# The stack's fills issued piece by piece in the attention stages of a two-layer model kernel

## What is computed

```python
x = L0_attn_x                                   # 16 x 256 x 128
xn = _layernorm(x)
s = _L0_attn_ref(xn, ...)                       # causal, 16 heads, the difference of two softmaxes, head norm
g = _silu(_L0_ffn_ref(xn, ...))                 # 8 experts, top 2, with a capacity
x = x + s * g
xn = _layernorm(x)
s = _L1_attn_ref(xn, ...)                       # 16 heads, a window of 128, with biases
g = _silu(_L1_ffn_ref(xn, ...))                 # 8 experts, top 2
x = x + s * g
```

## Time and profile before

| what | us |
|---|---|
| time, three executions | 1351.52, 1352.54, 1356.94 |
| median | 1352.54 |
| span of the profiled execution, first to last instruction | 1353.5 |
| attention of layer 0, from its first instruction | about 231 to 790 |
| attention of layer 1 | about 979 to 1353 |

### The profile page before, as it was taken

One profiled execution on the slowest core, in us unless ns is written; L12 is line 12 of the kernel. 1 busy time (PEld: TensorE's weight loads), 2 busy tenths in 40 slices (PEclk: granted clock), 3 DMA queues, 4 the chain that ended last, 5 costly groups with the idle time before them and its releaser, 6 DMA issues. The chain is left out here.

```text
span 1353.5 us, 38128 instructions
## 1 busy us (share of the span) xinstructions
PE 1071.2 (79%) x12376; PEld 808.5 (60%) x12376; DVE 809.8 (60%) x1668; ACT 799.8 (59%) x1892; POOL 615.5 (45%) x918
## 2 busy tenths in 40 slices
PE   4359998588999798899987344999857888978885
PEld 3349998355565455556554244999824655655553
DVE  4676664568777577777751357666436664755641
ACT  4845555057777677777776342655514665656663
POOL 6256553023455456555665416655303242444443
PEclk9999999579999899999998555999958898989997
DMA  6402222322332222232200340222212122222210
GB/s 181 113 24 69 70 69 47 93 56 58 85 77 58 58 57 65 67 85 68 57 20 9 94 109 16 71 69 68 55 47 63 44 64 66 55 62 64 52 48 20
DMA packets 144615, 86.43 MB, mean 64 GB/s; under 512 B 16547, under 2 KB 138037, under 8 KB 144469
## 3 DMA queue, kind: packets, MB, share of 16 engines
q1 hardware_dynamic: 135828, 66.72, 18.9%
q0 software_dynamic: 8640, 17.71, 5.6%
HBM read 30.06 MB, written 15.60 MB: 34 GB/s over the span
## 5 line engine op out<-in xcount | busy, mean ns | idle before, releaser
L1424 DVE TENSOR_REDUCE at_maxima<-ps 128x2 f32<-128x512 f32 (+1 forms) x576 | 371.7, 683 | 226.3 <-PE ps L1117 223.9
L1313 ACT ACTIVATE at_probs<-ps 128x512 f32<-128x512 f32 x576 | 320.8, 598 | 108.8 <-PE ps L1117 104.2
L1116 PE MATMUL ps<-tables 64*128 64x256 bf16 (+1 forms) x2304 | 229.6, 260 | 128.9 <-DMA stack<-at_pieces 62.3
L1117 PE MATMUL ps<-stack 62*128 62x256 bf16 (+3 forms) x3072 | 265.6, 255 | 2.4 <-issue 2.4
L717 ACT ACTIVATE ex_hid<-ps,ex_w 128x128 f32<-128x128 f32 x568 | 162.0, 368 | 120.3 <-PE ps L690 111.2
L1116 PEld LDWEIGHTS ps<-tables 64*128 64x128 bf16 x2304 | 91.7, 96 | 229.7 <-issue 193.9
L646 POOL DMA_INDIRECT ex_rows<-xn_rows,ex_ids_now x142 | 143.7, 1012 | 110.4 <-PE ps L681 68.7
L1117 PEld LDWEIGHTS ps<-stack 62*128 62x128 bf16 (+1 forms) x3072 | 167.1, 99 | 13.7 <-issue 2.6
L750 DVE COPY ex_w<-weights 128x1156 f32 x142 | 109.3, 769 | 103.8 <-issue 102.8
L1005 POOL DMA_INDIRECT at_chosen_y<-list_out,at_slot x128 | 130.1, 1017 | 55.3 <-issue 29.0
L690 PE MATMUL ps<-ex_rowsT,ex_w 128*128 128x128 f32 x1136 | 154.8, 281 | 0.0
(11 more groups left out here) (188 smaller groups left out, 1504.2 us busy)
## 6 DMA issues: line engine op xcount, KB each, us to landing
stack<-at_pieces SPq DMA_DIRECT2D x192, 128.0 KB, 2.7
stack<-at_pieces SPq DMA_DIRECT2D x192, 64.0 KB
list_out<-ex_result SPq DMA_DIRECT2D x142, 64.0 KB, 1.5
weights<-in_L_w SPq DMA_DIRECT2D x4, 1024.0 KB, 5.6
weights<-in_L_w SPq DMA_DIRECT2D x16, 256.0 KB, 6.6
xn_rows<-xn SPq DMA_DIRECT2D x8, 512.0 KB, 3.3
ex_rows<-xn_rows,ex_ids_now POOLq DMA_INDIRECT x142, 2.6
x<-in_L_attn_x SPq DMA_DIRECT2D x4, 512.0 KB, 6.1
```

The costliest lines, as they stand in the source:

```text
L1116: return nc.tensor.matmul(fine(bank, j), R.eye[tile, j, :], mask[tile], start=(j == 0), stop=True, skip_group_check=(j > 0))
L1117: return nc.tensor.matmul(bank[:, j - 2, :], left(j - 2)[tile], right(j - 2)[tile], start=False, stop=True, skip_group_check=True)
L1313: nc.scalar.activation(probs[:, (n // 3) % 2, n % 3, i * 512:(i + 1) * 512], t_bank[i], ACT.Exp, scale=SCALE).then_inc(t_free, 1)
L1424: nc.vector.tensor_reduce(by_half[:, h0:h0 + heads, a], s_bank[i].rearrange("p (m k) -> p m k", k=P * (late + 1)), AX.X, ALU.max).then_inc ...
```

## The change

SyncE no longer issues the twelve DMAs of a fill together behind the third piece. `fill_stack` becomes `fill_pieces`, called three times a step. Piece 0's six DMAs wait for ScalarE's copy of the second projection (`g_free`), and for all DMAs of earlier fills (`stacked`). Piece 1's four wait for VectorE's second split operation (`split_chain`), piece 2's two for the third (`pieces_ready`). In layer 1 piece 0 stands ahead of the shift in SyncE's order, in layer 0 behind it; in layer 1 the store comes between pieces 1 and 2. The other engines' programs stay as they are.

```diff
-            def fill_stack(b, r):
+            def fill_pieces(step, b, r, piece):
 
                 pieces = pieces_of[r % 2]
-                lone_wait(sp, t_full, (b - 3) * BANKS)
-                lone_wait(sp, pieces_ready, b + 1)
-                for j in (0, 4, 1, 5, 2, 3):
-                    which = Q_PIECE[j], K_PIECE[j]
-                    for tensor in range(2):
-                        src = pieces[:, which[tensor]].rearrange("p (a t) s -> p a t s", t=2)[:, :, tensor, :]
+                if piece == 0:
+                    lone_wait(sp, t_full, (b - 3) * BANKS)
+                    lone_wait(sp, stacked, b * LOADS)
+                    lone_wait(sp, g_free, use(step, "qk1") + 1)
+                elif piece == 1:
+                    lone_wait(sp, split_chain, b * 2 + 2)
+                else:
+                    lone_wait(sp, pieces_ready, b + 1)
+                for tensor, rows_of in ((0, Q_PIECE), (1, K_PIECE)):
+                    for j in range(len(rows_of)):
+                        if rows_of[j] != piece:
+                            continue
+                        src = pieces[:, piece].rearrange("p (a t) s -> p a t s", t=2)[:, :, tensor, :]
                         dst = stack[r % DEEP][j:P:STEP].rearrange("p h (a t) s -> p h a t s", t=2)[:, :, 0:A, tensor, :]
                         sp.dma_start(dst, src).then_inc(stacked, 16)
...
             def body(step, r):
+                fill, ahead = has(step, "split"), (step, step + SPLIT_AHEAD, r + SPLIT_AHEAD)
+                if layer and fill:
+                    fill_pieces(*ahead, 0)
                 if has(step, "shift"):
                     fill_shift(step + 1, r + 1)
-                if has(step, "split"):
-                    fill_stack(step + SPLIT_AHEAD, r + SPLIT_AHEAD)
+                if not layer and fill:
+                    fill_pieces(*ahead, 0)
+                if fill:
+                    fill_pieces(*ahead, 1)
                 if has(step, "out") and layer == 1:
                     store(step - 2)
+                if fill:
+                    fill_pieces(*ahead, 2)
             schedule(sp, body)
```

## The result

| | before | changed |
|---|---|---|
| time, median | 1353.94 us (4 runs, 1351.52 to 1356.94) | 1300.09 us (4 runs, 1298.88 to 1300.54) |
| span of the profiled execution | 1353.5 us | 1298.1 us |
| ratio | | 0.9596, 95% interval 0.9575 to 0.9616 |

The change makes the kernel 4.0% faster. The forecast was 1299 us with a range of 1288 to 1323.

The account below looks back on a forecast made before the run. It took SyncE's issue time for the stack's fill, which TensorE awaits in layer 1, as the bound. 29.4 + 1.9 + 10.8 + 3.3 + 11.2 - 2.0 = 54.6 us off 1353.5 gave 1299 us, range 1288 to 1323.

Parts of the forecast that it names:

- The bound: Layer 1, unit 3: TensorE waits 50.3 us in all for the stack's DMAs, a wait for SyncE's issue time.
- The steady waits, -29.4 us: Layer 1, steps 2 to 13: fill 6.4 to 7.2 us earlier, so all waits at unit 3 go, saving 29.4 us.
- The start of layer 1, -1.9 and -10.8: First fill's issues begin sooner, saving 1.9 us; the waits in steps -1, 0 and 1 go, saving 10.8 us.
- Layer 0, -3.3: Layer 0's first fill: issues begin 3.3 us sooner, saving 3.3 us; steady steps costed at nothing.
- The reason that I gave: Layer 0's first fill: 12 issues at 0.64 us take longer than the splitting, so the earlier start saves 3.3 us.
- The clock, -11.2: Layer 1 steps: of ten clock falls at waits, 1.5 us each, 7.5 go, saving 11.2 us (bounds 0 and 14.9).
- The shift behind piece 0, +2: Layer 1, unit 0: the shift's two DMAs, now behind six issues, cost 0.15 us in 13 steps, +2 us (bounds 0 and 13).
- the room reckoned at 0.6 us: Layer 1, unit 0: TensorE could go on the shift at 1159.0 and needs it at 1159.63, leaving 0.6 us.
- The rival's mechanism: Slower kernel: the shift held behind piece 0 in SyncE's order costs more than all waits removed; about 1366 us, chance 0.02.
- The end, 0: From the shift of step 13 to the kernel's end: no change forecast, 0 us.
- the sum: Whole kernel: all gains less the shift's cost, 54.6 us off the profiled 1353.5 us.
- The rule that spoke against the change: Layer 1 fill: issue time usually small beside the DMA, so nothing much happens; about 1350 us, 1353 by the rule, chance 0.03.

Follow-up runs that it names:

- the series 0, 2, 4 and 10 early issues: Changed kernel with only 2 or 4 of layer 1's fill DMAs issued early: 1321.6 and 1304.5 us; 0 is the kernel before (1353.9), 10 the changed one (1299.2).
- the kernel with this part alone: Kernel before with the new fills in layer 0 only, layer 1 keeping the old ones: ratio 0.9971, 3.9 us faster.
- the filled waits: Kernel before with ten matmuls of 512 columns added in layer 1 just ahead of TensorE's wait for the stack: ratio 0.9922, 1343.4 us.
- the late shift: Changed kernel with the shift's DMAs moved behind piece 1 as well in layer 1's SyncE order: ratio 0.9929, 1344.3 us.
- a second issuing queue: Changed kernel with one split operation moved to unit 4, plus ScalarE issuing six key DMAs of each layer's first fill: 1291.3 us, ratio 0.9535.

## Why the prediction held

**The bound.** The wait at unit 3 of layer 1 was one for SyncE's issues. Shown by the series 0, 2, 4 and 10 early issues: the waits shrink with each, and with two early their mean is 1.45 us where 1.4 had been worked out from the 0.64 us of an issue.

**The steady waits, -29.4 us.** All gone.

**The start of layer 1, -1.9 and -10.8.** Measured 2.2 and 11.2, in the second profile 2.2 and 10.0.

**Layer 0, -3.3.** The first fill brought 3.4 us up to the next projections (233.22 to 298.56 before, 232.92 to 294.87 changed), and the kernel with this part alone was 3.9 us faster. The trace has 1.6 us more in layer 0 and the experts. That needs no effect of the change. The trace before has a low clock at 722 to 732 us that the first trace of the changed kernel does not have, but the second one does. In order: before, changed, changed again.

```profile
722.00:732.00 10.00, 9.46 (x84) 4.98 (x88) 0.00 (x0) 6.01 (x14) 6.79 (x15) 0.53 0.11 28
...
722.00:732.00 10.00, 7.63 (x108) 4.75 (x109) 1.04 (x2) 6.00 (x14) 6.20 (x9) 1.00 0.11 28
...
722.00:732.00 10.00, 9.63 (x92) 5.45 (x84) 0.29 (x1) 5.71 (x13) 6.24 (x12) 0.55 0.11 28
```

With it the changed kernel comes to layer 1 at 979.22 us and not at 976.34, so executions of one kernel differ here by more than the 1.6 us. Over all runs, the three traces with the old fill in layer 0 all have this low clock and reach layer 1 at 979.9 to 982.7 us; of the ten with the new fill five have it (977.4 to 979.5) and five have it briefly or not at all (976.3 to 977.8). Whether the new fill makes it rarer is not shown. The reason that I gave was incomplete: in this layer the issues and the transfers take the same time, about 200 GB/s.

**The clock, -11.2.** I let a quarter of ten falls come back. Two came back in the profiled run of the changed kernel (near 1040 and 1194 us), a third stands at the loop's pause as before. A second profile of the same kernel had five outside the pause, and a span 2.0 us longer. Of the eleven falls outside the pause before, nine or six went. So 7.5 was a fair middle, and the count differs from one execution to the next. That most of them come with idle waits is shown by the filled waits, and from the other side by the late shift. The Trainium skill's rule (TensorE: Matmul & The Clock Gate, "HAM oscillation"), by which all ten would go, held for most of them and not for all. The kernel in that section waits longer than this one does in most steps; here waits of 1.6 to 3.5 us had a fall each in the run with the late shift.

**The shift behind piece 0, +2.** It was 0.4 us, a single wait. The size was too large by 1.6 us, and the room reckoned at 0.6 us was enough in every step but one. With four more DMAs ahead of it the same wait comes to 31.7 us. The rival's mechanism is real, and takes effect one group later than the change goes.

**The end, 0.** In the first trace of the changed kernel it is 3.6 us longer, in the second 0.2 us shorter than before. The stretch from 20.9 to 33.9 us behind the shift of step 13, first trace, then second:

```profile
1258.00:1271.00 13.00, 13.00 (x96) 7.13 (x94) 0.00 (x0) 6.24 (x13) 5.20 (x10) 0.50 0.10 26
...
1264.00:1277.00 13.00, 10.79 (x134) 6.83 (x133) 1.57 (x5) 9.69 (x21) 7.45 (x13) 1.00 0.11 30
```

The clock stood at 1.2 GHz through it in one execution and at 2.4 GHz in the other, of the same kernel. So the 3.6 us come from the execution and not from the change.

**Luck.** That the sum came within 1 us of the span is in part luck. In the first profile 1.7 us of gain more than forecast up to layer 1 and 2.7 us more in its steps up to 13 stood against 3.6 us less at the end. In the second the sum of 54.6 stands against 53.4, without so large an error in any row.

**The rule that spoke against the change.** The Trainium skill (DMA: Bandwidth & Descriptors, "Issuing engines are not separate DMA queues") calls the issue time usually small beside the DMA. For the 64 KB DMAs of layer 1 the measurement decides against it, since a second issuing queue doubled the rate; for the 128 KB DMAs of layer 0 it agrees as far as that a second queue gained nothing (wait 9.2 and 9.3 us).

## What to carry to other kernels

When an engine waits for a batch of small DMAs, count how many issues stand between the last input and the semaphore, times the pitch of an issue: that product, not the data, can be the wait, and it goes once the DMAs whose data are ready earlier are issued earlier. A few early issues, up to the room of the step, give most of the gain. Before moving issues forward on an in-order queue, reckon the room of what they now stand ahead of, because a group too many there cost 45 of the 55 us; and add the clock's price to each idle wait of TensorE that goes or comes.

## What was not expected of the hardware

The rate of one queue doubled with the DMA's size: 98 GB/s at 64 KB, 200 GB/s at 128 KB, with nearly the same pitch (0.64 and 0.67 us). Two queues gave 195 and 185. Filling TensorE's idle waits with ten useless matmuls each made the kernel 0.8% faster, with no other change. With the late shift the 13 waits of 1.6 to 3.5 us came with a fall of the clock each, while the clock fell five times where the 12 waits were 0.3 to 3.0 us, 1.45 in the mean. And two executions of one kernel differ in where the clock falls: five times against two in the steps, and 13 us at 1.2 GHz at the end against none.
